# A decoder layer on one core: two blocks made one, weight preparation as a chain of jobs in the engines' lists

## The reference, cut to what matters

```
# 1: attention to a memory of 256 rows, 8 heads of 128, three steps
Q = layernorm(x) @ Wq.T;  K, V = layernorm(memory) @ Wk.T, ... @ Wv.T
xi = Q per head
for _ in range(3):
    w = entmax15((xi @ K.T) * exp(log_beta));  xi = w @ V
x = norm(x + concat(xi) @ Wo.T)
# 2: latent cross attention, 16 heads; kv_rope is a rotated context of width 64
scores = (x @ xWq.T @ w_kc_q @ W_qr) . (kv_rope @ W_kr)
x = norm(x + (softmax(scores) @ kv_rope @ w_kc_kv.T) @ xWo.T)
# 3
x = norm(x + x @ (weight * scale).T + bias)
```

## Time and profile before

| | us |
|---|---|
| three runs, median | 923.12 |
| profiled execution, its own time | 923.41 |
| its span in the profile | 921.6 |
| TensorE busy | 839.4 (91%) |
| VectorE busy | 784.1 (85%) |
| ScalarE busy | 712.9 (77%) |
| GpSimd busy | 490.8 (53%) |
| loads and stores | 17.54 MB, nearly all in the first 50 us |

### The profile page before, as it was taken

One profiled execution on the slowest core, in us unless ns is written; L12 is line 12 of the kernel. 1 busy time (PEld: TensorE's weight loads), 2 busy tenths in 40 slices (PEclk: granted clock), 3 DMA queues, 4 the chain that ended last, 5 costly groups with the idle time before them and its releaser, 6 DMA issues.

```text
span 921.6 us, 16971 instructions
## 1 busy us (share of the span) xinstructions
PE 839.4 (91%) x4958; PEld 725.2 (79%) x4958; DVE 784.1 (85%) x2053; ACT 712.9 (77%) x1694; POOL 490.8 (53%) x2278
## 2 busy tenths in 40 slices
PE   4988887597999999999999999999999999999972
PEld 3866776476888888888888888888988888877852
DVE  1646798999999999999999999999999999988431
ACT  1535698999879789989898989898989898877320
POOL 3002324655465656656666575657666667655522
PEclk9999998898999999999999999999999999999986
DMA  8910000000000000000000000000100000000000
GB/s 256 275 47 1 12 1 1 1 4 7 4 1 1 1 2 0 5 1 1 1 28 1 1 1 2 1 1 1 36 2 1 2 12 1 1 1 1 19 5 20
DMA packets 24145, 17.54 MB, mean 19 GB/s; under 512 B 11696, under 2 KB 23472, under 8 KB 23792
## 3 DMA queue, kind: packets, MB, share of 16 engines
q1 hardware_dynamic: 23808, 16.13, 6.4%
q0 software_dynamic: 240, 0.27, 0.3%
HBM read 14.30 MB, written 2.10 MB: 18 GB/s over the span
## 4 chain that ended last, share of the span: by engine, by line
PE 74%; DVE 11%; ACT 5%; issue 2%; POOL 1%; POOLq 0%; ACTq 0%
PE banks L1209 32%; PE banks L1229 12%; PE banks L1220 8%; PE banks L1257 6%; PE banks L1290 6%; DVE moments L889 4%; PE banks L1266 3%; PE banks L1282 2%; DVE top L871 2%; ACT work L816 2%; PE banks L1114 2%; PE banks L1303 1%; DVE work L909 1%; ACT work L810 1%; PE banks L1273 1%
## 5 line engine op out<-in xcount | busy, mean ns | idle before, releaser
L889 DVE BATCH_NORM_STATS2 moments<-work 128x6 f32<-128x512 f32 x576 | 380.0, 687 | 8.2 <-ACT work L816 5.1
L1209 PE MATMUL banks<-weights_s,work 128*128 128x256 f32 x1536 | 360.7, 385 | 8.9 <-ACT work L805 4.4
L816 ACT ACTIVATE work<-work,neg_u 128x256 f32<-128x256 f32 x768 | 330.7, 514 | 40.2 <-DVE neg_u L904 23.9
L1209 PEld LDWEIGHTS banks<-weights_s,work 128*128 128x128 f32 x1536 | 288.0, 193 | 49.2 <-ACT work L805 5.5
L810 ACT ACTIVATE work<-banks,neg_low 128x256 f32<-128x256 f32 x384 | 154.8, 498 | 15.2 <-DVE neg_low L880 15.0
L871 DVE MAX8 top<-banks 128x8 f32<-128x256 f32 x384 | 142.5, 416 | 19.0 <-PE banks L1209 17.8
L1220 PE MATMUL banks<-ident,work 128*128 128x128 f32 x768 | 114.8, 282 | 27.9 <-DVE work L909 21.7
L990 POOL TENSOR_TENSOR resid_sum<-moments 128x8 f32<-128x8 f32 x144 | 30.4, 211 | 192.7 <-DVE moments L889 191.7
L828 ACT ACTIVATE work<-banks 128x512 f32<-128x512 f32 x192 | 112.8, 607 | 23.6 <-PE banks L1220 23.2
L1220 PEld LDWEIGHTS banks<-ident,work 128*128 128x128 f32 x768 | 91.8, 145 | 47.2 <-DVE work L909 27.9
L1229 PE MATMUL banks<-weights_s,work 128*128 128x256 f32 x512 | 117.8, 384 | 0.0
(11 more groups left out here) (157 smaller groups left out, 1151.9 us busy)
## 6 DMA issues: line engine op xcount, KB each, us to landing
rows<-in_x_dram SPq DMA_DIRECT2D x1, 2048.0 KB, 15.6
work<-in_L_xattn_Wq_dram SPq DMA_DIRECT2D x1, 2048.0 KB, 15.6
work<-in_L_xattn_Wo_dram SPq DMA_DIRECT2D x1, 2048.0 KB, 13.8
out_dram<-work SPq DMA_DIRECT2D x16, 128.0 KB, 1.8
work<-in_L_xattn_w_kc_q_dram SPq DMA_DIRECT2D x1, 1536.0 KB, 15.4
work<-in_L_attn_Wq_dram SPq DMA_DIRECT2D x1, 1024.0 KB, 12.5
work<-in_L_attn_Wo_dram SPq DMA_DIRECT2D x1, 1024.0 KB, 16.9
work<-in_ctx_dram SPq DMA_DIRECT2D x32, 32.0 KB, 2.1
```

Source lines behind the costliest of these rows:

```text
L816: ins = nc.scalar.activation(q_resid[:, j, h, :], q_resid0[:, j, h, :], ACT.Relu, bias=small["neg_u"][:, j, h:h + 1])
L889: ins = nc.vector.bn_stats(moments[:, j, 2 * q:2 * q + 2, :].rearrange("p h k -> p (h k)"), r.rearrange("p h n -> p n h"))
L1209: ins = nc.tensor.matmul(ps_scores[:, h, :], lhsT, w[:, h, t, :], start=(t == 0), stop=(t == CT - 1))
```

## The change

The first block is gone; all is one block. The preparation is one chain of 76 jobs (`prep_jobs`), which stand in the lists of the tiles. Score_in comes ahead of Wv's jobs, the chain's later part (from ffn_t on) mixes value_out with the latent jobs, and the last of them stands in TensorE's list behind the first score quarters of step 2 of tile 0. `prep_bank` gives jobs 0 to 14 all eight banks, 15 to 28 three (5 to 7), and the rest two (6 and 7). Even jobs are copied by ScalarE, odd ones by VectorE. A tile's first stages wait for the weights they use, head by head, and not for a block.

Loads stand in another order: memory, Wk, two small columns, Wq, the first four tiles of x, Wv, Wo, ffn, xWo, and so on; w_kc_q comes in two halves, and tiles 4 to 15 of x come last, behind job a2, because twelve heads of xWq lie in their place until then. Buffers of raw weights are laid out anew. The statistics of x are made by four tiles at a time: VectorE's x_stats, and GpSimd's x_rstd in seven instructions for four tiles in place of a square root on ScalarE; norm_in waits for its group. The memory's norm, GpSimd's constants and the ffn scaling are stages of the lists too (mem_norm, setup, ffn_scale).

All five lists of turns are written anew, also where no preparation stands. In GpSimd's, worst_all now stands behind the second normalise of tile f, followed by rstd 2 of tile c, rstd 1 of tile f, rstd 2 of tile d, bias of f, rstd 2 of e and rstd 2 of f; VectorE's worst stands behind the second sum of tile f, and flag last.

```diff
-    made = [("late", x, 0, 0) for x in range(len(late_jobs()))]
-    out = [[("late_out", x, 0, 0) for x in range(which, len(made), 2)] for which in range(2)]
-    return {"PE": [pe, [], made], "DVE": [dve, once("worst") + once("flag"), out[0]], "ACT": [act, [], out[1]],
-            "POOL": [pool, once("worst_all"), once("diag_zero")], "SP": [once("fetch") + once("store"), [], []]}
+    made = [("prep", x, 0, 0) for x in range(len(prep_jobs()))]
+    out = [[("prep_out", x, 0, 0) for x in range(which, len(made), 2)] for which in range(2)]
+    x_stats, x_rstd = ([(name, b, 0, 0) for b in range(TILES // 4)] for name in ("x_stats", "x_rstd"))
+    dve_out = once("mem_norm") + out[1][:3] + x_stats[:1] + out[1][3:11] + once("ffn_scale") + out[1][11:] + x_stats[1:]
+    return {"PE": [pe, [], made], "DVE": [dve, once("worst") + once("flag"), dve_out], "ACT": [act, [], out[0]],
+            "POOL": [pool, once("worst_all"), once("setup") + x_rstd + once("diag_zero")],
+            "SP": [once("fetch") + once("store"), [], []]}
...
 def prep_jobs():
 
     jobs = [("wk_t", i) for i in range(2)] + [("mem_t", 0)] + [("k_t", i) for i in range(4)]
+    jobs += [("score_in", h) for h in range(HEADS)]
     jobs += [("wv_t", i) for i in range(2)] + [("v_t", i) for i in range(4)]
-    jobs += [("score_in", h) for h in range(HEADS)]
     jobs += [("score_step", h) for h in range(HEADS)]
-    jobs += [("wo_t", i) for i in range(4)]
-    jobs += [("value_out", h) for h in range(HEADS)] + [("ffn_t", 0)]
+    jobs += [("wo_t", i) for i in range(4)] + [("ffn_t", 0)]
+    for i in range(4):
+        jobs += [("xwo_t", 2 * i), ("value_out", 2 * i), ("xwo_t", 2 * i + 1), ("value_out", 2 * i + 1), ("b", i)]
+    jobs += [("kcq_t", 0), ("wkr_t", 0), ("kcq_t", 1), ("wkr_t", 1)]
+    for i in range(4):
+        jobs += [("n", i)] + [("kcq_t", 2 * i + 2)] * (i < 3) + [("m", i)] + [("kcq_t", 2 * i + 3)] * (i < 3) + [("a", i)]
     return jobs
 
 
-def late_jobs():
-
-    jobs = [("wkr_t", i) for i in range(2)]
-    for i in range(4):
-        jobs += [("kcq_t", 2 * i), ("kcq_t", 2 * i + 1), ("n", i), ("xwo_t", 2 * i), ("m", i), ("xwo_t", 2 * i + 1),
-                 ("a", i), ("b", i)]
-    return jobs
+def prep_bank(x):
+
+    if x < 15:
+        return x % 8
+    return 5 + x % 3 if x < 29 else 6 + x % 2
...
-        with nc.Block() as block:
...
-                for n, (kind, i) in enumerate(jobs):
-                    if n % 2 != which:
-                        continue
-                    eng.wait_ge(prep_filled, n + 1)
-                    bank = banks[:, n % 8, :]
...
-                    if which == 1 and kind == "score_step":
-                        x_stats(eng, ld_x, range(i // 2 * 4, i // 2 * 4 + 4))
...
-                                                    ALU.mult).then_inc(ffn_scaled_ready, 1)
-                        eng.wait_ge(x_stats_ready, 4)
-                        row_norms(eng, 0, norm_step, tile_var_ready, tile_std_ready)
-                    if which == 0 and (kind, i) == ("wo_t", 3):
-                        row_roots(eng, 0, tile_var_ready, tile_std_ready)
...
+            def made_by(eng, kind, i):
+
+                eng.wait_ge(prep_filled, job_no[(kind, i)] + 1)
+
+            def emptied_of(eng, kind, i):
+
+                x = job_no[(kind, i)]
+                eng.wait_ge(prep_emptied[x % 2], x // 2 + 1)
+
+            def prep_out(eng, x):
+                (kind, i), bank = jobs[x], banks[:, prep_bank(x), :]
...
+                def load_heads(part):
+                    heads = slice(HEADS * part, HEADS * (part + 1))
+                    sp.dma_start(kcq_raw, w_kc_q.rearrange("h k q -> k h q")[:, heads, :]).then_inc(ld_kcq, 16)
+
+                def load_rows(tiles, done):
+                    sp.dma_start(rows[:, HID * tiles.start:HID * tiles.stop].rearrange("p (t c) -> p t c", c=HID),
+                                 x.rearrange("(t p) c -> p t c", p=P)[:, tiles, :]).then_inc(done, 16)
+
+                sp.dma_start(mem_raw, memory.rearrange("(t p) c -> p t c", p=P)).then_inc(ld_mem, 16)
+                sp.dma_start(wk_raw, Wk.rearrange("(h p) c -> p h c", p=P)).then_inc(ld_wk, 16)
+                for col, src in ((gm_col, g_mem), (bm_col, b_mem)):
+                    sp.dma_start(col[:, :], src.rearrange("(t p) -> p t", p=P),
+                                 allow_slow_non_contiguous=True).then_inc(ld_affine, 16)
+                sp.dma_start(wq_raw, Wq.rearrange("(h p) c -> p h c", p=P)).then_inc(ld_wq, 16)
+                load_rows(slice(0, 4), ld_x_first)
+                sp.dma_start(wv_raw, Wv.rearrange("(h p) c -> p h c", p=P)).then_inc(ld_wv, 16)
+                sp.dma_start(wo_raw, Wo.rearrange("(t p) c -> p t c", p=P)).then_inc(ld_wo, 16)
+                sp.dma_start(ffn_raw, ffn_w.rearrange("(t p) c -> p t c", p=P)).then_inc(ld_ffn, 16)
+                for t in range(CT):
+                    sp.dma_start(xwo_raw[t], xWo[P * t:P * (t + 1), :]).then_inc(ld_xwo, 16)
+                sp.dma_start(kckv_raw, w_kc_kv.rearrange("h k d -> k h d")).then_inc(ld_kckv, 16)
+                sp.wait_ge(pad_ready, 1)
+                src = W_kr.rearrange("(g two) d r -> d g two r", two=2)
+                for odd in range(2):
+                    at = slice(XD * odd, XD * (odd + 1))
+                    sp.dma_start(wkr_pad[at, :, at], src[:, :, odd, :]).then_inc(ld_wkr, 16)
+                load_heads(0)
+                sp.dma_start(wqr_raw[0:QS, :, :, :], W_qr.rearrange("h (t q) r -> q h t r", q=QS)).then_inc(ld_wqr, 16)
+                src = xWq.rearrange("(h p) c -> p h c", p=P)
+                sp.dma_start(xwq_raw[0], src[:, 0:12, :]).then_inc(ld_xwq, 16)
+                sp.dma_start(xwq_raw[1], src[:, 12:XH, :]).then_inc(ld_xwq, 16)
+
+                made_by(sp, "kcq_t", 3)
+                load_heads(1)
+
+                made_by(sp, "a", 2)
+                load_rows(slice(4, TILES), ld_x_rest)
...
                         act.wait_ge(top_step[j], p * (3 * STEPS) + (3 * s + 3))
+                        if (p, j, s, q) == (0, 1, 0, 0):
+
+                            made_by(act, "v_t", 3)
...
+                        if (p, j, s, e, q) == (0, 1, 0, 1, 0):
+
+                            made_by(act, "wo_t", 3)
...
+                        dve.wait_ge(x_rstd_step, X_OPS * (p + 1))
+                        if (p, j) == (0, 1):
+
+                            made_by(dve, "mem_t", 0)
+                        if (p, j) == (0, 3):
+
+                            made_by(dve, "b", 3)
...
+                    elif stage == "x_stats":
+                        x_stats(dve, ld_x_rest if s else ld_x_first, range(4 * s, 4 * s + 4))
+                        dve.wait_ge(x_stats_ready, s + 1)
+                        for t in range(4 * s, 4 * s + 4):
+                            ins = nc.vector.bn_aggr(tile_mv[:, t, :], tile_stats[:, t, :])
+                        ins.then_inc(x_mean_ready, 1)
+                    elif stage == "ffn_scale":
+                        dve.wait_ge(ld_ffn, 16)
+                        dve.wait_ge(ld_small, 16 * N_SMALL)
+                        for t in range(CT):
+                            nc.vector.tensor_scalar(ffn_scaled[:, t, :], ffn_raw[:, t, :], ffn_s[:, t:t + 1], None,
+                                                    ALU.mult).then_inc(ffn_scaled_ready, 1)
                     elif stage == "residual":
...
+                    elif stage == "x_rstd":
+                        at = slice(4 * s, 4 * s + 4)
+
+                        def step(n):
+                            return X_OPS * s + n
+
+                        pool.wait_ge(x_mean_ready, s + 1)
+                        nc.gpsimd.tensor_tensor(tile_var[:, at], tile_mv[:, at, 1], eps_col[:, :], ALU.add).then_inc(x_rstd_step, 1)
+                        pool.wait_ge(x_rstd_step, step(1))
+                        nc.gpsimd.tensor_tensor(x_guess[:, at], tile_var[:, at], minus_half[:, :], ALU.pow).then_inc(x_rstd_step, 1)
...
+                    elif stage == "setup":
+                        nc.gpsimd.memset(ident[:, :], 0.0).then_inc(setup, 1)
+                        pool.wait_ge(setup, 1)
+                        nc.gpsimd.affine_select(out=ident[:, :], in_=ident[:, :], compare_op=ALU.not_equal, fill=1.0, base=0,
+                                                pattern=[[-1, P]], channel_multiplier=1).then_inc(ident_ready, 1)
+                        for col, src in ((g_col, g_state), (b_col, b_state), (ffn_s, ffn_scale)):
+                            pool.dma_start(col[:, :], src.rearrange("(t p) -> p t", p=P),
+                                           allow_slow_non_contiguous=True).then_inc(ld_small, 16)
+                        nc.gpsimd.memset(wkr_pad, 0.0).then_inc(pad_ready, 1)
...
+                def bank_of(what):
+
+                    stage, s, _, q = what
+                    if stage == "prep":
+                        return prep_bank(s)
+                    if stage == "scores":
```

(49 more changed lines are left out.)

587 lines of the change are left out of this document (261 added, 326 removed).

## The result

After the change a run takes 907.46 us (median of 906.23 to 909.65), before 923.12 (921.08 to 924.58): ratio 0.984, 95% interval 0.982 to 0.986. The profiled execution of after took 906.48, its span 904.6. The kernel is faster by 15.7 us; the forecast was 27. The stated range of 885 to 914 held it; the forecast's own part of it, 887 to 903, did not. That distance is what the experiments are about.

What follows compares the result with a forecast made beforehand. TensorE (98%) and VectorE (95%) were taken as full from 215.8 to 850 us, with losses at both ends. Start and ramp -35.5, behind A +4, tail +3.5 from 923.4 gave 895.4, said as 896 us; range 885 to 914.

Steps and rivals of the forecast that it cites:

- Start: Kernel start: first job at about 7.4 us, first top of tile 0 at 24.3, 30.8 us earlier than 55.07.
- Second part of the ramp: First weights of tile 0 to A: VectorE 113 us of work, 93% busy, so 121.4 us; TensorE about 113.
- A: First weights of step 2 of tile 0 in VectorE's list, ending the ramp: from 215.16 to 179.7 us, 35.5 earlier.
- rival 1: TensorE takes over in the ramp: 133 us in place of 121, A at 191, total 907; chance 0.12.
- the rule weighed in the prediction: Ramp: a TensorE kept waiting between bursts is throttled, so interleaved jobs would run slow, about what rival 1 costs.
- Loads: Ramp: VectorE waits 0 to 2 us for tiles 4 to 15 of x, loaded behind job a2; at worst 10.
- rival 3: Early start doesn't carry: x comes late (6 us) and the x_rest wait costs 10; total 912; chance 0.08.
- Behind A: Steady part after A: both lists hold nearly the same; leftover work costs +4 us, bounds -8 and +20.
- Rival 2: Steady part: new lists are worse, 2 points of TensorE's 98% cost 13 us, total 909; chance 0.10.
- the rival on the slower side: Between A and 850 us VectorE loses its 95%; below 91% the gain is gone, at 90% 928; chance 0.08.
- Tail: Kernel end: moved GpSimd reduction, two gaps near 6 us, delays rstd 1 of tile f: +3.5 us, -3.8 to +9.

Runs made afterwards that it cites:

- the mirror: The kernel before, its own lists kept up to tile 0's first step-2 weights, the new order behind (F: those weights of last tile f): 948.20 us, ratio 1.027.
- the best splice: The kernel after with the reduction on TensorE, its new lists up to 220 us and the order of before behind: 883.83 us, ratio 0.960 to before.

## Why the prediction was right, and where it was off

**Direction and range.** Faster (0.88) and 885 to 914 held. The forecast of 896 lay 11.5 us too low, and 907.46 is outside the forecast's own 887 to 903 (0.58): the range held it only because it reached out to the rivals. One term was wrong by more than 20 us; two others came out better by 12 together, and that they hid half of it is luck.

**Start.** First work 6.64 (forecast 7.4), first top 25.51 (24.3), first weights of tile 0 57.8 (58.3): right within 1.2 us.

**Second part of the ramp: better than forecast, 116.3 us for 121.4.** VectorE's work was right (138.8 us from the first top to A, forecast 140); the share of 93%, taken from before, was too low: 112.04 of 116.25 is 96.4%. TensorE's work was taken too large, 113 us for 102.8 measured; 79.7 of the 113 came from a stretch at a granted clock of 0.90, and what that share of the difference is was not separated. With 88% busy TensorE didn't take over, and rival 1 fell. It was also wrong where it named the clock: the granted clock rose from 0.90, in a stretch without jobs, to 0.99 in one that has them, 1.00 up to 136 us and 0.96 behind the last job; with all jobs moved ahead it was 0.84. This is the other side of the rule weighed in the prediction (the Trainium skill, "TensorE: Matmul & The Clock Gate", "HAM oscillation"): the waits throttle, and the jobs remove the waits.

**Loads.** The first x load was waited for 0.43 us and the second 0.34, within the 0 to 2; rival 3 fell.

**Behind A: +4 forecast, +26.7 measured. This is the step that failed.** "Both lists hold nearly the same" was right for the work and was taken as right for the time. The order of the new lists, put at nothing in the sum, costs 26.3 us in this stretch with no early start at all (666.14 for 639.84, the mirror). What the +4 stood for, the work that an earlier A leaves over, is then about 0.4 (666.55 for 666.14); in the best splice A to F takes 4.8 more than before, but its joint is in that. Rival 2, a worse order, is what happened; I gave it 0.10 and 13 us. Its total of 909 was near 907.46 because the ramp and the tail came out better, not because of its price: the order costs some 24 us net of the tail, of which a joint of the two orders gave back 12 to 15. It named TensorE's share, 2 points of 98%; that fell by 1.1 (645.52 of 666.55 is 96.8%), above the 96% that was to show the forecast wrong. TensorE and VectorE were also busy longer, which a busy share doesn't show: VectorE by 10 us over the same number of instructions. Its share fell to 93.9% between A and F, not to the 91% of the rival on the slower side. One guess at why the chance was too low: a list that is rewritten throughout against a stretch at 98% and 95% has little to win and much to lose.

**Tail: +3.5 forecast, -2.6 measured.** Two terms in one. The mechanism was right, two gaps of 5.72 and 7.59 us with rstd 1 of tile f behind them, and the reduction costs 7 to 8 us in the new order (907.46 to 900.23; 906.68 to 898.55, on two chips) and 5.2 in the old (896.78 to 891.63, also on two chips). What I left out is that a new order also moves work across F: 7.6 us of TensorE's.

**Sum.** Forecast 923.4 - 35.5 + 4 + 3.5. By span: 921.6 - 41.1 + 26.7 - 2.6 = 904.6. The forecast is 893.6 in the same measure (1.8 less than by time). The 11.0 us between are 22.7 behind A, less 5.6 of the ramp and 6.1 of the tail.

## What to carry to other kernels

Preparation that fills the waits of a latency-bound ramp can be free, as it was here, even where an average says that the engine is full: count what the ramp's own chains leave idle, at the clock that they leave. An order that already keeps two engines at 95% and 98% is an asset of its own: forecast a rewrite of it as a cost until a stretch shows otherwise, and change only the part that the edit needs, joining old and new where they stand at the same depth. To price an order by itself, play it behind an unchanged start and compare the same two points of the work, not the same times. A cross-lane reduction on GpSimd in a tail is priced by the gaps around it, not by its row.

## What the runs showed of the hardware

- The partition_all_reduce of 0.38 us was surrounded by gaps of 5.55 to 5.80 us before and 6.87 to 7.59 behind in the kernel before and in every version that had it, wherever it stood; both were gone when a copy stood in its place. The Trainium skill, "GPSIMD Engine Reference", "Instruction dispatch", has one such load of about 6 us for the first call; here the return to ordinary instructions costs one too.
- VectorE's small SCALAR_TENSOR_TENSOR (128x8, L805) takes 0.12 to 0.17 us where it meets no instruction of GpSimd (17 of 48 in the kernel after) and up to 1.00 where it starts beside GpSimd's 128x512 normalise that is under way, and ends with it:

```profile
615.59 0.99 DVE L805 SCALAR_TENSOR_TENSOR neg_u<-delta,neg_limit 128x8 f32<-128x8 f32 x1
```

```profile
615.51 1.04 POOL L1007 TENSOR_TENSOR work<-work 128x512 f32<-128x512 f32 x1
```

Its mean is 283 ns in the new order and 215 in the last kernel, 3 us over all 48. The Trainium skill, "GPSIMD Engine Reference", "Specifications", says that GpSimd's SBUF interfaces are shared with VectorE and contended when VectorE's instruction has two SBUF inputs, as this one has; the trace agrees (9 of the 48 took 0.60 to 1.00 us, each beside a 128x512 or 128x256 instruction of GpSimd).
- TensorE's mean granted clock in the ramp followed its waits: 0.84 and 0.90 in stretches without jobs (busy 70% and 77%), 0.99 with them (88%); within the latter 1.00 up to the last job (busy 75.2 of 78.2 us) and 0.96 behind it (27.5 of 38.0). It is no fixed property of a list: with the same lists 130 to 174 us was granted 0.88, 0.92 and 0.96 to 0.98 in different runs.
